# One gathered tile per chunk replaced by 64 single-row loads on the sync engine and 64 column copies on ScalarE

## The reference

```python
h = jnp.maximum(_layernorm(x, axis=-1), 0.0)                 # [12500, 128]
hcat = jnp.concatenate([h[src], h[dst], edge_attr_32], -1)   # [400000, 288]
m = jax.nn.relu(hcat @ w1 + b1) @ w2 + b2                    # a message for each edge
agg = jax.ops.segment_sum(m, dst, num_segments=12500)
gi, gh = agg @ w_ih + b_ih, h @ w_hh + b_hh                  # [12500, 384] each
i_r, i_z, i_n = jnp.split(gi, 3, -1); h_r, h_z, h_n = jnp.split(gh, 3, -1)
r, z = sigmoid(i_r + h_r), sigmoid(i_z + h_z)
n = tanh(i_n + r * h_n)
out = x + (1.0 - z) * n + z * h
```

## Time and profile before

| what | value |
|---|---|
| median of 3 runs | 4001.66 us (4000.51 to 4002.24) |
| time of the profiled execution | 4009.54 us |
| its span, first to last instruction | 4007.8 us |
| PE / DVE / ACT / POOL busy | 75% / 43% / 32% / 75% of the span |
| mean granted TensorE clock | 0.870 |
| DMA traffic | 287.99 MB, mean 72 GB/s |

### The profile page before, as it was taken

The page is one execution under the profiler, slowest core; times in us unless marked ns, Lnnn a source line. Parts: engine busy times, 40 slices in busy tenths (PEclk is TensorE's granted clock), DMA queues, the critical chain, the costliest instruction groups (busy, mean ns, idle before and its releaser), DMA issues.

```text
span 4007.8 us, 76313 instructions
## 1 busy us (share of the span) xinstructions
PE 2996.9 (75%) x20157; PEld 2691.1 (67%) x20157; DVE 1716.2 (43%) x6014; ACT 1281.7 (32%) x3575; POOL 2991.4 (75%) x3163
## 2 busy tenths in 40 slices
PE   5777777777777777777777777777777777777777
PEld 4667666667666666666666667666666666766666
DVE  6444444444444444444444444444444444444443
ACT  5333333333333323333333333333333333333332
POOL 4777777777777777777777777777777777777776
PEclk8888889888888888888888888888888888888887
DMA  6222222222222222222222222222222222222222
GB/s 187 68 69 69 69 69 69 69 69 70 69 69 69 70 70 69 69 69 70 69 69 69 69 69 70 69 69 69 70 69 69 69 69 69 69 69 69 69 69 56
DMA packets 275619, 287.99 MB, mean 72 GB/s; under 512 B 153847, under 2 KB 204696, under 8 KB 275475
## 3 DMA queue, kind: packets, MB, share of 16 engines
q0 software_dynamic: 100000, 205.00, 20.4%
q1 hardware_dynamic: 147282, 69.63, 6.1%
q10 hardware_dynamic: 28318, 13.14, 1.2%
HBM read 274.60 MB, written 12.83 MB: 72 GB/s over the span
## 4 chain that ended last, share of the span: by engine, by line
POOL 71%; issue 26%; DMA 1%; POOLq 1%; DVE 1%; PE 1%; ACT 0%; SPq 0%; DVEq 0%; ACTq 0%
POOL rows L423 71%; POOLq L227 1%; DMA p_rows<-low 1%; POOLq L238 0%; DMA acc<-in_x_dram 0%; DVE stats L700 0%; PE ps L1032 0%; PE ps L1005 0%; DVE mv L706 0%; DVE dst_int L779 0%; DMA onehot<-base_f_dram 0%; DVE low L725 0%; PE ps L1093 0%; PE ps L1094 0%; ACT low L505 0%
## 5 line engine op out<-in xcount | busy, mean ns | idle before, releaser
L423 POOL DMA_INDIRECT rows<-p_rows,idx x3125 | 2960.9, 947 | 964.4 <-issue 952.3
L574 ACT ACTIVATE lhs<-ps 96x640 f32<-96x640 f32 x625 | 437.6, 700 | 2590.5 <-PE ps L1008 2585.4
L1032 PE MATMUL ps<-onehot,rows 128*128 128x95 f32 x6250 | 915.1, 298 | 427.0 <-ACT rows L580 425.9
L1032 PEld LDWEIGHTS ps<-onehot,rows 128*128 128x128 f32 x6250 | 830.6, 210 | 520.9 <-ACT rows L580 290.4
L800 DVE TENSOR_TENSOR rows<-rows,ps 128x640 f32<-128x640 f32 x625 | 512.7, 820 | 1341.3 <-DMA rows<-p_rows,idx 1335.2
L1019 PE MATMUL ps<-rhs,lhs 128*128 128x128 f32 x6250 | 983.8, 315 | 68.9 <-DVE rows L800 68.4
L1019 PEld LDWEIGHTS ps<-rhs,lhs 128*128 128x128 f32 x6250 | 919.0, 229 | 97.2 <-issue 89.9
L1005 PE MATMUL ps<-ident,onehot 128*96 128x128 f32 x3125 | 547.6, 315 | 475.0 <-DVE onehot L790 473.8
L1005 PEld LDWEIGHTS ps<-ident,onehot 128*96 128x96 f32 x3125 | 385.6, 145 | 567.7 <-DVE onehot L790 560.2
L790 DVE TENSOR_SCALAR onehot<-iota_w,dst_int 128x95 f32<-128x95 f32 x3125 | 736.1, 298 | 51.1 <-issue 51.0
L580 ACT ACTIVATE rows<-rows 128x640 f32<-128x640 f32 x625 | 460.0, 736 | 84.6 <-DVE rows L800 82.1
(11 more groups left out here) (94 smaller groups left out, 1307.9 us busy)
## 6 DMA issues: line engine op xcount, KB each, us to landing
rows<-p_rows,idx POOLq DMA_INDIRECT x3125
lhs<-in_ea_t_dram SPq DMA_DIRECT2D x625, 80.0 KB
idx<-in_src_cols_dram SPq DMA_DIRECT2D x625, 2.5 KB
p_rows<-low SPq DMA_DIRECT2D x14, 448.0 KB, 3.6
x_fin<-in_x_dram ACTq DMA_DIRECT2D x123, 50.0 KB
out_dram<-out_fin ACTq DMA_DIRECT2D x123, 50.0 KB
acc<-in_x_dram SPq DMA_DIRECT2D x13, 448.0 KB, 4.8
low<-in_dst_rows_dram SPq DMA_DIRECT2D x1, 1562.5 KB
```

The lines of the kernel that those rows point to most:

```text
L423: pool.indirect_dma_start(out=rows[:, s, t, :], out_offset=None, in_=p_rows[:, :], in_offset=bass.IndirectOffsetOnAxis(ap=idx[:, s, t:t + ...
L574: nc.scalar.activation(lhs[0:WB, s, :], onehotT_ps, ACT.Copy, accum_out=count[:, s:s + 1])
L1032: nc.tensor.matmul(sg[:, 0:W], rows[:, s, t, :], onehot[:, s, t, 0:W], start=(t == 0), stop=(t == T - 1))
```

## The change

Tile 24 of each chunk (group 4, tile 4: `LAST`, `T - 1`) is no longer gathered by POOL. Of its 128 edges, the first 64 are served by SP: for each it reads the node number into a register, and loads that node's row of `p_rows` into a partition of `picked_rows` (64 DMAs of 512 bytes, in four lots of 16 behind the loads of groups 1 to 4). The other 64 are served by ACT: for each it reads the node number into a register and copies that column of `hT` into a column of `picked` (64 copies of 128x1, in four lots of 16 in steps 1 to 4). PE adds both to the tile's pre-activation in PSUM: `picked` times the source rows of w1 (`w1_keep`, columns 0 to 63 of `picked` are zero), and a product with the identity, which adds `picked_rows`. ACT then applies relu from PSUM straight to the message buffer (`relu_direct`), so DVE's add and ACT's relu of group 4 cover four tiles. The node numbers of these tiles are turned into 16-bit numbers and laid in one partition row in setup. Four times a chunk SP, and four times ACT, read 16 of them in one call, without a check of their range. The rest of the diff keeps the counts of the semaphores right and shares semaphores with `general()`.

```diff
+PICKED_TILE = G * T - 1
+HALF = P // 2
+PICK = 16
+PICKS = HALF // PICK
+PICK_FROM = G - PICKS
+LAST = G - 1
+def gather_tiles(s):
+    return T - 1 if s == LAST else T
...
             sp.dma_start(dst_nat, dst_rows).then_inc(dstn_in, 16)
+            sp.dma_start(w1_keep[:], w1[0:D, :]).then_inc(weights_in, 16)
+            sp.dma_start(pick_nat[0:CHUNKS, :], src_tiles.rearrange("(c k) p -> c k p", k=G * T)[:, PICKED_TILE, :]).then_inc(dstn_in, 16)
...
+            def pick_rows(c, k):
+
+                if k == 0:
+                    sp.wait_ge(pick_in, 32)
+                    wait(sp, pre_ready[LAST], c)
+                _, nodes = nc.values_load_multi_w_load_instructions(
+                    pick_sp[0:1, bass.ds(c * HALF + k * PICK, PICK)], (mybir.EngineType.SP,), min_val=0, max_val=N - 1,
+                    skip_runtime_bounds_check_because=IN_RANGE)
+                for j, node in enumerate(nodes):
+                    e = k * PICK + j
+                    sp.dma_start(picked_rows[e:e + 1, :], p_rows[bass.ds(node, 1), :]).then_inc(picked_rows_in[k], 16)
+
             def chunk(c):
                 for s in range(G):
                     load_group(c, s)
+                    if s >= PICK_FROM and not (isinstance(c, int) and c == 0):
+                        pick_rows(c, s - PICK_FROM)
                 if isinstance(c, int) and c == 0:
...
+                    sp.wait_ge(ranges_ready, 1)
+                    sp.wait_ge(w2ih_copied, 2)
+                    for half, row in enumerate((pick_sp, pick_act)):
+                        sp.dma_start(row.rearrange("o (c e) -> o c e", e=HALF),
+                                     pick_half[0:CHUNKS, half * HALF:(half + 1) * HALF]).then_inc(pick_in, 16)
+                    sp.wait_ge(pick_in, 32)
                     sp.dma_start(deg[0:1, 0:N], acc[0:1, 0:N]).then_inc(deg_zeroed, 16)
+                    for k in range(PICKS):
+                        pick_rows(0, k)
...
-                    for t in range(T):
+                    for t in range(gather_tiles(s)):
                         pool.indirect_dma_start(
...
+            def pick_columns(c, k):
+
+                if k == 0:
+                    act.wait_ge(pick_in, 32)
+                    wait(act, pre_ready[LAST], c)
+                _, nodes = nc.values_load_multi_w_load_instructions(
+                    pick_act[0:1, bass.ds(c * HALF + k * PICK, PICK)], (mybir.EngineType.Activation,), min_val=0, max_val=N - 1,
+                    skip_runtime_bounds_check_because=IN_RANGE)
+                for j, node in enumerate(nodes):
+                    e = HALF + k * PICK + j
+                    last = nc.scalar.copy(picked[:, e:e + 1], hT[:, bass.ds(node, 1)])
+                last.then_inc(picked_act, 1)
+
+            def relu_direct(c):
+
+                act.wait_ge(pre_ready[LAST], c + 1)
+                wait(act, seg_ready[LAST], c)
+                nc.scalar.activation(rows[:, LAST, T - 1, :], pre_ps[LAST % 2][:, (T - 1) * D:T * D], ACT.Relu).then_inc(direct_ready, 1)
+
             def relu_message(c, s):
                 act.wait_ge(summed[s], c + 1)
-                m = rows[:, s, :, :]
+                m = rows[:, s, 0:gather_tiles(s), :]
...
                     copy_onehot(c, s)
+                    old = before(c, s, 1)
+                    if s == 0 and old:
+                        relu_direct(old[0])
                     if s + 1 < G:
 
                         copy_window(c, s + 1)
                     old = before(c, s, 2)
                     if old:
                         relu_message(*old)
+                    if s >= PICK_FROM:
+                        pick_columns(c, s - PICK_FROM)
...
-            dve.wait_ge(dstn_in, 16)
+            dve.wait_ge(dstn_in, 32)
+            nc.vector.tensor_copy(pick_half[0:CHUNKS, :], pick_nat[0:CHUNKS, :])
...
+            nc.vector.memset(picked[:, 0:HALF], 0.0).then_inc(ones_set, 1)
...
                     pe.wait_ge(summed[old[1]], old[0] + 1)
+                    if s == 0:
+                        pe.wait_ge(direct_ready, old[0] + 1)
...
+                    direct = t >= gather_tiles(s)
                     last = nc.tensor.matmul(pre_ps[s % 2][:, t * D:(t + 1) * D], lhs[:, s, t * P:(t + 1) * P],
-                                            rhs[:, s, :], start=True, stop=True)
+                                            rhs[:, s, :], start=True, stop=not direct)
+                    if direct:
+                        pe.wait_ge(ones_set, 2)
+                        pe.wait_ge(picked_act, (c + 1) * PICKS)
+                        last = nc.tensor.matmul(pre_ps[s % 2][:, t * D:(t + 1) * D], picked[:], w1_keep[:], start=False, stop=False)
+                        for k in range(PICKS):
+                            pe.wait_ge(picked_rows_in[k], (c + 1) * (PICK * 16))
+                        last = nc.tensor.matmul(pre_ps[s % 2][:, t * D:(t + 1) * D], ident[0:HALF, :], picked_rows[:], start=False, stop=True)
                 last.then_inc(pre_ready[s], 1)
 
             def segment_sums(c, s):
 
                 pe.wait_ge(message_ready[s], c + 1)
+                if s == LAST:
+                    pe.wait_ge(direct_ready, c + 1)
```

More of the change, by code:

```diff
@@ L10 @@
 I32 = mybir.dt.int32
+U16 = mybir.dt.uint16
 P = 128
@@ L53 @@
 LN = LAG * FN
+PICKED_TILE = G * T - 1
[4 more added lines that the diff above has]
+LAST = G - 1
+IN_RANGE = "src holds node indices, 0 to N - 1"
+def gather_tiles(s):
+    return T - 1 if s == LAST else T
 D = 128
@@ L104, in gnn_kernel @@
         at += GROUPS
+        pick_nat = low[:, at:at + P].bitcast(I32)
+        at += P
+        pick_half = low[:, at:at + HALF].bitcast(U16)
+        at += HALF
         assert at <= NPAD
+        pick_sp = low[2 * ED:2 * ED + 1, 0:CHUNKS * HALF // 2].bitcast(U16)
+        pick_act = low[3 * ED:3 * ED + 1, 0:CHUNKS * HALF // 2].bitcast(U16)
         dst_int = sb("dst_int", [P, GROUPS * T], I32)
@@ L115, in gnn_kernel @@
         w1_dst = sb("w1_dst", [P, D])
+        w1_keep = sb("w1_keep", [P, D])
+        picked = sb("picked", [P, P])
+        picked_rows = sb("picked_rows", [HALF, D])
         idx = sb("idx", [P, G, T], I32)
@@ L211, in gnn_kernel @@
         fin_chain = sem("fin_chain")
+        pick_in, picked_act, direct_ready = (sem(n) for n in ("pick_in", "picked_act", "direct_ready"))
+        picked_rows_in = sems("picked_rows_in", PICKS)
         g_zeroed, g_mask_set, g_scattered, g_chain, g_b1_in = (sem(n) for n in ("g_zeroed", "g_mask_set", "g_scattered", "g_chain", "g_b1_in"))
         g_h_ready, g_q_ready, g_q_copied, g_q_stored = (sem(n) for n in ("g_h_ready", "g_q_ready", "g_q_copied", "g_q_stored"))
-        g_src_in, g_dst_in, g_ea_in = (sem(n) for n in ("g_src_in", "g_dst_in", "g_ea_in"))
+        g_src_in, g_dst_in = (sem(n) for n in ("g_src_in", "g_dst_in"))
         g_gathered = sems("g_gathered", 3)
-        g_bc_ready, g_bcT_ready, g_pre_ready, g_summed, g_message_ready, g_seg_ready, g_new_ready = (sem(n) for n in (
-            "g_bc_ready", "g_bcT_ready", "g_pre_ready", "g_summed", "g_message_ready", "g_seg_ready", "g_new_ready"))
+        g_bc_ready, g_bcT_ready, g_new_ready = (sem(n) for n in ("g_bc_ready", "g_bcT_ready", "g_new_ready"))
+        g_ea_in, g_pre_ready, g_summed, g_message_ready, g_seg_ready = (v[0] for v in (
+            ea_in, pre_ready, summed, message_ready, seg_ready))
         g_sums_in, g_sumsT_ready, g_sumsT_kept = (sem(n) for n in ("g_sums_in", "g_sumsT_ready", "g_sumsT_kept"))
@@ L309, in load_indices @@
             def load_indices(c, s):
-                wait(sp, rows_in[s], c * (16 * T))
+                wait(sp, rows_in[s], c * (16 * gather_tiles(s)))
                 sp.dma_start(idx[:, s, :], src_cols[bass.ds(c * (G * P) + s * P, P), :]).then_inc(idx_in[s], 16)
@@ L431, in general @@
                 for s in range(G):
-                    pool.wait_ge(rows_in[s], 16 * T)
+                    pool.wait_ge(rows_in[s], 16 * gather_tiles(s))
                 nc.gpsimd.memset(g_zero, 0.0).then_inc(g_zeroed, 1)
@@ L645, in fast @@
                 over_chunks(act, chunk)
+                relu_direct(CHUNKS - 1)
                 for back in (2, 1):
@@ L653, in general @@
                 for s in range(G):
-                    act.wait_ge(rows_in[s], 16 * T)
+                    act.wait_ge(rows_in[s], 16 * gather_tiles(s))
                 def q_tile(j):
@@ L795, in add_pre @@
             def add_pre(c, s):
+                k = gather_tiles(s)
                 dve.wait_ge(pre_ready[s], c + 1)
-                dve.wait_ge(rows_in[s], c * (16 * T) + 16 * T)
-                r = rows[:, s, :, :].rearrange("p t f -> p (t f)")
-                nc.vector.tensor_tensor(r, r, pre_ps[s % 2], ALU.add).then_inc(summed[s], 1)
+                dve.wait_ge(rows_in[s], c * (16 * k) + 16 * k)
+                r = rows[:, s, 0:k, :].rearrange("p t f -> p (t f)")
+                nc.vector.tensor_tensor(r, r, pre_ps[s % 2][:, 0:k * D], ALU.add).then_inc(summed[s], 1)
```

(2 more changed lines are left out.)

4 lines of the change are left out of this document (2 added, 2 removed).

## The result

| | before | after |
|---|---|---|
| median | 4001.95 us (4000.51 to 4002.27, 4 runs) | 6147.41 us (6142.79 to 6159.88, 4 runs) |
| ratio, 95% interval | | 1.537 (1.534 to 1.539) |
| span of the profiled execution | 4007.8 us | 6141.0 us |
| PE / DVE / ACT / POOL busy | 75 / 43 / 32 / 75% | 66 / 27 / 34 / 47% |
| mean granted TensorE clock | 0.870 | 0.675 |

The kernel became 2145 us slower. Forecast were 3862 us and a range that ends at 4600. Some 96 us of each kernel lie before the first gather and behind the last one (76 and about 20 in the kernel before), so a chunk takes (time - 96) / 125: 31.25 us before, 48.4 after.

The account below looks back on a forecast made before the run. POOL's gathers were taken to bound the kernel. The terms -156.4 + 9.7 (start) + 7 (ring) + 0.5 gave -139 us, so 3870 us profiled and 3862 us as median; the range was 3838 to 4600.

Parts of the forecast that it names:

- the start: In chunk 0 all 64 picks stand ahead of an index load on SP, so POOL stands 9.7 us, once.
- the ring: SP's picks and PE's product wait for each other across chunks: 30.1 us a chunk, level with POOL's 30.04; costs about 7 us.
- what a gather fewer is worth: On POOL, one of 25 gathers a chunk goes: 1.2515 us x 125 = 156.4 us, leaving 30.04 us a chunk.
- R, the read of 16 numbers: Register read at the head of each lot: taken as 0.48 us, bounds 0.29 and 4.6; called the weakest term.
- Rival 2: On SP, register reads are priced by the number, so the kernel gets slower: about 4765 or 5915 us; chance 0.22.
- SP's pick: One row's DMA with its address on SP: 0.36 us, bounds 0.29 and 0.54; 64 make 23.0 us a chunk.
- rival 3: On SP, a pick costs more than 0.38 us: about 4580 us at 0.45, 5300 at 0.54; chance 0.12.
- the landing: Time until a DMA's rows arrive on SP's ring: 1.8 us; the loads of groups 0 and 1 (2.1 us) fit in.
- rival 4: ACT becomes the bound, only with copies at 0.24 us and reads above 1 us; chance 0.06.
- About 1 us of the lot sticks out: In the round of PE and ACT, 3.9 us a group hides most of a 2.9 us lot: 23.5 us a chunk.
- All engines are late together: ACT's wait at relu_direct in step 0 adds nothing of its own; late picks delay every engine, already counted in the ring.
- PE beside idle time: PE's four added instructions, 0.5 us a chunk beside 9 us idle, cost nothing; uncovered, 62 us.

Follow-up runs that it names:

- e5: The kernel after, with relu_direct in ACT's step 0 moved behind the window copy and the relu of group 3: 6001 us.
- e6: The kernel after without reads (fixed rows and columns picked) and with relu_direct moved behind the window copy and the relu of group 3: 4309 us.
- e10: e6 with each lot of 16 rows loaded on SP by one DMA in place of 16; ACT's 64 copies kept: 4132 us.
- e11: e10 with ACT's four lots of copies moved to the end of their steps, behind sigmoid and tanh: 3849 us.
- e2: The kernel after without reads on SP and ACT; all 64 DMAs and 64 copies stay, of fixed nodes: 4642 us.
- e3: The kernel after with reads on SP alone; ACT copies fixed columns without reads: 5968 us.
- e1: The kernel after, with the four lots' numbers read in reads of 1, 4, 8 and 16 numbers on SP and ACT: 6515 us.
- e8: The kernel after with the direct relu late and each lot's 16 numbers read as eight 32-bit words, split in registers: 5082 us.
- e4: The kernel after with reads on ACT alone; SP loads fixed rows without reads: 6124 us.
- e13: e8 with ACT's lots moved to the end of their steps: 5072 us.
- v_alternate2: Against the kernel before: picks in every second chunk, lots of 8, direct relu late, ACT's lots last, reads of four 32-bit words: 3927.05 us, ratio 0.981.
- e15: The version picking in every second chunk with 16-bit reads, lots of 8 (4420 us), with ACT's lots moved to the end of their steps: 4063 us.

## Why the prediction was wrong

Taking the causes away one by one leads from the kernel after to the forecast: direct relu late (e5) -146 us, no reads (e6) -1692, one DMA a lot (e10) -177, lots last on ACT (e11) -283. The sizes hold in this order; taken first, the reads are worth 1505 (e2). What is left, 3849 us, lies 13 below the forecast of 3862. That is not the forecast come true, as e11 has neither reads nor 64 picks on SP. It confirms POOL's part alone: 3862 less the 9.7 and 7 us put down for the start and the ring is 3845.

- **POOL, and what a gather fewer is worth: right.** Gathers stayed 1.25 us apart, 24 in 30.0 us (e11). The 156 us were there to be had. In the kernel after POOL stood 3207 us, of which the 0.30 us at each gather are 914, as in e11.
- **R, the read of 16 numbers: the step that failed.** "I take 0.48, the dearer single read, since the 32 bytes lie side by side." It measured 3.43 us, seven times that, and lay within the upper bound of 4.6. On SP that is 4 x 2.95 = 11.8 us a chunk. Rival 2 had named the mechanism and the place and stood at 0.22. That its figures came so near (46.6 us and 5915, where e3 had 46.9 and 5968) is partly luck: its read of 4.6 us was too dear by 4.7 us a chunk, and the rest of the sum, below, too cheap by 4.8. The Trainium skill's "Runtime: NRT & Kernel Launch", section "Instruction fetch mechanics", says that a register load from HBM costs some 200 ns a register even in bulk. Here the loads are from SBUF: e1's 0.21 us per further 16-bit number agrees, and e8's 32-bit words, 0.70 us for eight, do not. The row with 0.476 beside 0.287 was read as a sign that the count matters little. It was none: in the kernel after the same read of one number has a median of 0.452.
- **SP's pick: 0.36 forecast, 0.404 measured, and the ring without reads: 28.2 us forecast, 33.0 measured (e6).** The DMA was right (0.228 for 0.22), the rest was 0.176 for 0.14, both within a lot of the kernel after. That is 2.8 us a chunk, and past the 0.38 at which rival 3 decides. In e6 the lots take 26.4 us where 23.0 were put down, and the rest 6.6 where 5.2 stood for three loads, landing, product and signal. Where the prediction let the loads of groups 0 and 1 fit into the landing, SP's queue in e3 never waits at all, so all five groups' loads and the gaps count: its own work sets the pace, not the ring through PE. With the reads, 33.0 + 4 x 3.43 = 46.8 us, which is e3's 46.9. So the forecast would have failed without the reads too: e6, which has none, took 4309 us, e10, which has no 64 issues on SP either, 4132.
- **The reads on ACT and ACT's round: wrong.** ACT's busy time per chunk was 16.4 us, with 4 x 3.5 us of reads beside it; that is at most 30.4 of 48.4 us, so it was not the bound as an engine (rival 4). "About 1 us of the lot sticks out", a round of 23.5 us, failed. The 3.9 us a group came from a stretch at the start where no nodes are finished yet, so gates, candidate and update were not in it, and a lot was costed by its length and not by what stands behind it. With 1.6 us lots the round was 32.3 us in e10; with the reads, and the direct relu early, 48.2 in e4.
- **`relu_direct` costed at nothing: wrong.** 2.7 us a chunk without reads (e2 against e6). "All engines are late together" missed that the relu of the group before was queued behind it.
- **PE beside idle time: right for its instructions, wrong for its clock.** PE had time for four instructions more. But in a chunk full of gaps the granted clock was 0.64 for 0.89 and PE's work took 33.5 us for 21.9; over whole runs it was 0.675 for 0.870, and 0.903 in e11, where the gaps are gone. How much of the period the clock made and how much it merely followed was not separated.
- **The start: 9.7 us forecast, 29 measured,** the reads and picks again (36.8 us and the first read before them, for 23 + 1.9). The prediction's own terms give 116.5 for the index load, not 116.8, which changes nothing. In e11, with no picks to speak of, nothing of it is left; in the sum it is 19 us of 2145.

## What to carry to other kernels

A term that no row shows, and that four instructions a chunk multiply on a queue with no slack, decides the case: measure it by itself, in the form it will have (count, width, engine), before anything is built on it. On an in-order queue cost a new piece of work by what stands behind it: the same 64 copies a chunk cost 283 us with their lots ahead of the sigmoid and the tanh (e10), and nothing behind them (e11). A sum that comes out level with the bound leaves nothing for the gaps that no row shows; doing the work half as often, here in every second chunk, made the same idea 1.9% faster, all that the removed gathers were worth.

## What the runs showed of the hardware

- A read of several numbers from SBUF into registers costs 0.21 us for each further 16-bit number (0.25, 0.88, 1.74, 3.43 us for 1, 4, 8, 16 on SP; 3.55 for 16 on ACT). The first number is no dearer than a 32-bit one (0.287 us on ACT before); the further ones are. In 32-bit words a read took 0.464 us for four and 0.696 for eight on SP, 0.058 a further word. Storing the node numbers as 32-bit words was not tried; by these it would be about 0.70 + 8 x 0.058 = 1.2 us for 16 (an estimate).
- The read of one number on ACT had a median of 0.287 us in the kernel before, in e2 and in e3, and 0.452 in the kernel after and in e4, where ACT's reads of 16 run too; with reads of words beside it, it was 0.455 (e13) and 0.462 (`v_alternate2`).
- A gather by POOL costs 0.90 us for 64 rows and 0.94 for 128, and 0.30 between two.
- Copies of 128x1 on ACT take 0.187 us each, and follow each other every 0.093 us.
- PE's five transposes took 0.71 us at a granted clock of 1.00, before and after, and 1.27 to 1.30 at 0.50: 1.30 after a wait of 4.3 us, and 1.27 right behind other products, at 3001.5.
- Where the instruction queue moves some 10 packets in each turn of a loop, ACT's queue stood 2.7 us and SP's 3.1 us behind the branch on average (e15); in `v_alternate2`, where it moves next to nothing, both stood 0.3 us at most.
